# Attention's k-by-v products as two 64 by 64 matmuls in two halves of the array's columns, in place of one 128 by 128

## The reference

```python
xn = _ln(x, ln_w, ln_b)
q = xn @ Wq + bq
k = xn @ Wk + bk + (1.0 - src_mask) * -1000000.0
q = softmax(q.reshape(b, t, h, dh), axis=-1)     # over a head's features
k = softmax(k.reshape(b, t, h, dh), axis=1)      # over the tokens
v = ((xn @ Wv + bv) * src_mask).reshape(b, t, h, dh)
att = einsum('bnhd,bnhl->bhdl', k, v)            # dh x dh for each head
y = einsum('bnhd,bhdl->bnhl', q, att).reshape(b, t, d)
hh = _ln(y, ln2_w, ln2_b) * (1.0 + scale) + shift   # scale, shift from emb
return x + silu(hh) @ W_out + b_out
```

## Time and profile before

| what | value |
|---|---|
| median of 3 runs | 836.76 us (836.5 to 837.15) |
| the profiled execution's own time | 837.29 us |
| its span, first to last instruction | 835.5 us |
| PE busy | 795.3 us, 95% |
| DVE, ACT, POOL busy | 691.0, 514.5, 432.1 us |
| mean granted TensorE clock | 0.986 |

### The profile page before, as it was taken

How to read it: one execution, slowest core, us unless ns; L and a number is a source line. 1 busy time by engine, 2 the same in 40 slices (tenths; PEclk the granted TensorE clock), 3 DMA queues, 4 the chain that set the end, 5 groups by cost and what they waited for, 6 DMA issues and landing times.

```text
span 835.5 us, 13821 instructions
## 1 busy us (share of the span) xinstructions
PE 795.3 (95%) x4871; PEld 409.6 (49%) x4871; DVE 691.0 (83%) x1409; ACT 514.5 (62%) x1004; POOL 432.1 (52%) x425
## 2 busy tenths in 40 slices
PE   4999779997999999999999999999999999999987
PEld 2446335463454555545454555555454555555453
DVE  6888767786898888998978889888888889788877
ACT  4975872852857677686866766475656566460622
POOL 2265573542664747767674654637264535534340
PEclk9999979998999999999999999999999999999999
DMA  9777297763774848868493949768593939476542
GB/s 321 261 167 226 44 255 219 130 142 120 133 174 107 157 165 161 230 121 188 94 207 95 185 135 151 191 133 184 95 207 100 178 126 174 117 139 140 89 114 76
DMA packets 291093, 130.53 MB, mean 156 GB/s; under 512 B 261296, under 2 KB 261680, under 8 KB 291024
## 3 DMA queue, kind: packets, MB, share of 16 engines
q1 hardware_dynamic: 288288, 125.27, 65.7%
q10 hardware_dynamic: 2736, 4.39, 1.5%
HBM read 47.74 MB, written 16.88 MB: 77 GB/s over the span
## 4 chain that ended last, share of the span: by engine, by line
PE 80%; DVE 11%; ACT 3%; DMA 2%; POOL 2%; issue 1%; SPq 0%; DVEq 0%; ACTq 0%; POOLq 0%
PE ring L500 72%; PE att_ps L500 4%; DMA sb_ht_parts<-sb_htok 1%; DVE sb_k_or_qt L976 1%; ACT sb_k_or_qt L1350 1%; DVE sb_q_sum L1033 1%; DVE sb_row_peak L823 1%; DMA sb_x<-in_x 1%; DVE sb_q_max L1009 1%; DVE ring L1011 1%; DVE ring L1006 1%; DVE ring L1052 1%; DVE sb_y_stats L1056 1%; POOL sb_x L1573 1%; PE film_ps L582 0%
## 5 line engine op out<-in xcount | busy, mean ns | idle before, releaser
L500 PE MATMUL ring<-sb_w_hi,sb_xt_parts 128*128 128x512 f16 x1024 | 310.5, 380 | 4.7 <-DVE sb_v_or_q L991 4.7
L500 PE MATMUL ring<-sb_w_lo,sb_xt_parts 128*128 128x512 f16 x512 | 194.6, 380 | 0.0
L500 PE MATMUL ring<-sb_w_hi,sb_ht_parts 128*128 128x512 f16 x512 | 158.1, 383 | 7.5 <-DMA sb_ht_parts<-sb_htok 5.8
L500 PEld LDWEIGHTS ring<-sb_w_hi,sb_xt_parts 128*128 128x128 f16 x1024 | 100.7, 98 | 131.5 <-issue 7.7
L1582 POOL TENSOR_TENSOR sb_htok<-sb_ht_parts,sb_htok 128x512 f16<-128x512 f32 x60 | 74.9, 1270 | 149.6 <-ACT sb_htok L1384 149.6
L500 PE MATMUL ring<-sb_xt_parts,sb_w_hi 128*128 128x512 f16 x496 | 147.8, 380 | 0.0
L1598 POOL TENSOR_TENSOR sb_tanh<-sb_v_or_q,sb_kq_hi 128x512 f16<-128x512 f32 x64 | 74.1, 1157 | 88.7 <-ACT sb_kq_hi L1414 88.2
L500 PE MATMUL ring<-sb_w_lo,sb_ht_parts 128*128 128x512 f16 x256 | 98.0, 383 | 0.0
L500 PE MATMUL ring<-sb_xt_parts,sb_w_lo 128*128 128x512 f16 x248 | 94.0, 379 | 0.0
L1045 DVE SCALAR_TENSOR_TENSOR sb_x<-ring,sb_down_o,sb_x 128x512 f32<-128x512 f32 x64 | 47.0, 749 | 47.1 <-PE ring L500 44.6
L500 PEld LDWEIGHTS ring<-sb_w_hi,sb_ht_parts 128*128 128x128 f16 x512 | 50.9, 99 | 67.1 <-issue 10.6
(11 more groups left out here) (228 smaller groups left out, 1477.1 us busy)
## 6 DMA issues: line engine op xcount, KB each, us to landing
out<-sb_x SPq DMA_DIRECT2D x14, 1024.0 KB, 4.4
sb_rows_now<-film_rows SPq DMA_DIRECT2D x16, 512.0 KB, 4.7
sb_x<-out SPq DMA_DIRECT2D x8, 1024.0 KB, 5.4
sb_x<-in_x SPq DMA_DIRECT2D x7, 1024.0 KB, 5.6
sb_mask_add<-mask_terms SPq DMA_DIRECT2D x15, 256.0 KB, 5.6
sb_w_stage<-in_L_cond_Wk SPq DMA_DIRECT2D x2, 1024.0 KB, 8.4
sb_w_hi<-in_L_cond_W_emb SPq DMA_DIRECT2D x1, 1536.0 KB, 13.0
sb_w_lo<-in_L_cond_W_emb SPq DMA_DIRECT2D x1, 1536.0 KB, 13.9
```

Source lines behind the costliest of these rows:

```text
L500: last = nc.tensor.matmul(out, lhs, rhs, start=(n == 0), stop=(n == len(pairs) - 1))
```

## The change

For the units 1 to 15 `attention` calls a new function in place of `product`. For each of the 12 pairs of operands it issues two matmuls: one takes the first 64 features of k and of v and writes the upper left 64 by 64 square of the block, the other takes the last 64 and writes the lower right one. The output partition (0 or 64) places them in the first and the second half of the array's columns. The other two squares of the block are no longer written in these units; they keep what the tensor held, and the multiplication by `blocks` takes them to zero as before. In a unit 48 loads of 128 columns with 48 matmuls of 128 columns become 96 loads of 64 columns with 96 matmuls of 64 columns. In layer 0 the stationary operand is k and the moving one v, in layer 1 the other way round, before and after. Nothing is moved: the order of all other instructions, the semaphores and the waits stay.

```diff
+HALF = P // 2
@@
+            def pairs_of_heads(c, pairs):
+
+                for n, (lhs, rhs) in enumerate(pairs):
+                    for j in range(2):
+                        g = slice(j * HALF, j * HALF + HALF)
+                        last = nc.tensor.matmul(att_ps[g, c, g], lhs[:, g], rhs[:, g], start=(n == 0), stop=(n == len(pairs) - 1))
+                return last
+
             def attention(u):
@@
                     left, right = (k_parts, v_parts_t) if layer_of(u) == 0 else (v_parts_t, k_parts)
-                    last = product(att_ps[:, c, :], split_pairs(*left, *right))
+                    last = pairs_of_heads(c, split_pairs(*left, *right))
                 last.then_inc(att_summed, 1)
```

## The result

The changed kernel is **faster** by 0.55%, a little, but clear of the noise: 832.51 us median of 7 runs (830.5 to 834.82) against 836.76 for the kernel before (7 runs, 835.73 to 838.75); the ratio is 0.9945, 95% interval 0.9926 to 0.9964. The forecast was 841.0 us, slower. The rival "half-width fp16 loads are quick" had said 823.5. So the sign was missed, and the rival that had the sign right promised three times as much as came.

A forecast was written before the change was run, and what follows sets the result against it. PE's unbroken chain of matmuls was taken as the bound. Attention was to go from 2.68 to 2.97 us a unit, said as +0.30; 14 units add 4.2 us, giving a median of 841.0 us, range 823 to 846.

The forecast's parts named there:

- half-width fp16 loads are quick: Rival for attention's loads: 0.43 ns a column, rounds of 31 ns, -0.95 us a unit, 823.5 us; chance 0.27.
- The bound and the units: PE's unbroken chain sets the end; each ns of attention counts in 14 of the 15 changed units.
- What costs nothing: Mask multiplication, cast and low part after attention: 0.3 us later, covered by 10.4 us of output matmuls.
- The halves at once: In attention, two 64-column tiles run fully in parallel, so a unit takes 48 rounds.
- What does a load of 64 columns take?: Attention's 64-column load sets each round: 56 to 58 ns, taken as 57.
- the fp32 end: Attention's fp16 loads were taken at the fp32 loads' 0.86 ns a column.
- What the pages gave for the load: By the skill pages, a 64-column load in attention takes 53 ns, so a round is at least that and nothing is gained.
- Going in and out: Switching to and from narrow tiles around attention costs 0.09 us in and 0.10 us out; lower bound 0.
- The sum for the kernel: 14 units times 0.30 us give 4.2 us more over the whole kernel; median 841.0 us.
- One after another: Rival: attention's 96 pairs run serially at 0.056 us each, +2.9 us a unit, 855 to 878 us; chance 0.12.
- doesn't show: Rival: attention rounds of 56 ns and switch costs only with fp32, 836.8 to 837.5 us; chance 0.09.
- 831 us of a slower issue: Weaker form of the quick-load rival: attention's instructions issue at some 12 ns, 2.3 us a unit, kernel near 831.

The follow-up runs named there:

- one place: Changed kernel, but layer 0 sends both 64-column halves to the same half of the array's columns and layer 1 uses four 32-column quarters; 861.64 us.
- The run with 32 and 64 fp16 columns: Changed kernel, but layer 0 loads 64 columns and streams 32, while layer 1 loads 32 and streams 64; 831.32 us.
- one turn less: Changed kernel with the later peak sums, but in units 1 to 15 a plain transfer replaces the turn of q's low part; 824.92 us, 0.9841.
- later peak sums: Changed kernel, with the matmuls summing a weight's peak behind the fourth output tile instead of the third in units 3 to 6; 828.68 us, again 829.60.
- block order: Changed kernel, but layer 0 issues the first half's 12 matmuls ahead of the second half's, and layer 1 streams all 128 columns per half; 840.39 us.

## Why the prediction was wrong

**The bound and the units.** That PE's chain sets the end was right for the kernel before; that each ns won in 14 units would arrive was wrong, and for the slower forecast it didn't matter. The part "What costs nothing" looked at mask, cast and low part of attention only, and named no room for what else runs beside it. It is there that a gain needs a row: how much earlier than needed does each other operand of the next step arrive?

**The halves at once: right.** 3.15 us in one place, 1.64 in two.

**What does a load of 64 columns take? This is the step that failed.** It took "the fp32 end", 0.86 ns a column and a round of 57 ns, "because today's short load is a feature of a full-width load". The run with 32 and 64 fp16 columns shows 0.47 ns a column, and the round is 31.5 ns. The value between the ends, 0.43 "if fp16 is simply twice as fast as fp32", was near it. The rows had the hint: the prediction itself says that fp16 streams at 0.42 ns a column and fp32 at 0.84. That the narrow loads of the earlier trace rows "all stand on the one line of 0.86" was true, but all of them are fp32. The reading of 16 ns for the columns of a full-width load holds: take the 15 ns of 32 columns off their load of 98 ns and 83 are left, against the 82 that the prediction had from fp32. So a full-width fp16 load lasts as long as one of 32 columns, while one of 64 columns takes 15 ns more.

**What the pages gave for the load.** The Trainium skill's page "TensorEngine Tiling (Array Packing)", section "Restrictions and Gotchas", excludes Fast Weight Load, a quicker way of loading weights, under column tiling. The trace agrees in that the 64-column load (113 ns) is longer than the full-width one (98 ns). The figure of columns / 1.2 ns of the Trainium skill's page "TensorE: Matmul & The Clock Gate", section "LDWEIGHTS (loading the stationary operand)", is 53 ns for 64 columns; here the whole round is 31.5 ns. The measurement decides: 0.83 ns a column is near the fp32 loads here (0.86), not the fp16 ones (0.47). What the runs bear out is the up to twice the speed of the Trainium skill's page "TensorEngine Tiling (Array Packing)", section "Overview", which the prediction held only as a rival: 2.68 to 1.64 us is 1.6 times.

**Going in and out: right in size.** In 0.09 us; out 0.12 us in unit 7 in the chain, and in the other units 0.07 us of start-to-start distance beyond a full-width matmul. It comes with fp16 on both sides, so it isn't a matter of fp32, and its lower bound of 0 falls. The sum for a unit in the fast rival was -0.95 us; 46.80 - 45.86 is -0.94.

**The sum for the kernel.** 14 x 0.94 = 13.2 us, as that rival said. The distances from attention to attention show where the profiled execution gives it back, each against the kernel before less 0.94: 0.1 us in unit 2, 2.8 in the units 3 to 5, 0.8 in unit 7 (46.67), 0.3 in unit 8 (46.16), 1.5 in unit 9 (47.47), 0.6 in unit 11 (46.45) and 0.8 in unit 14 (51.06). That is 6.9 of 13.2. The 6.3 that are left, and the 0.45 that were won ahead of unit 2 by the clock, are the 6.8 by which the span fell. The median fell by only 4.3, as the profiled execution was the quickest of its seven and the one before lay above its median; the others' traces weren't kept, so their share can't be placed.

**The rivals.** One after another is refuted, and so is "doesn't show". The 831 us of a slower issue (which leaves out the 0.24 us of going in and out) lies near the measured time by chance: a unit's attention took 1.64 us and not 2.3. The chance of 0.27 for faster was low for a step whose value was chosen between ends of 8 and 55 ns. The range of 823 to 846 held the time; it is the direction that was wrong.

**What stays open.** That the turning transfers bind behind unit 6 is shown, as one less brings every unit from 8 to 13 to 45.86 us. It isn't shown whether it is SyncE's time to issue them or the DMA engines' work that would have to shrink: the run with one turn less takes away both. A full-accuracy kernel with fewer turns wasn't tried. The version that beats both kernels with all of the computation is the changed kernel with the later peak sums, 828.7 and 829.6 us in two sets of runs, 0.990 of before.

## What to carry to other kernels

When an operation's cost lies between two ends, look for the same factor in a neighbouring row (here fp16 against fp32 in the stream) before taking either end. A gain on the bounding engine arrives only up to the room that every other chain of the loop has: write that room down, in us, for each operand of the next step, and expect the rest to come back as waits. And test a repair on the old kernel too: one that is worth little there and 4 us on the new one names what the change uncovered.

## What the runs showed of the hardware

Two column halves take loads and matmuls side by side, 96 pairs in 1.64 us, 17 ns a pair. Four quarters don't scale on: 192 pairs took 1.79 us at best in the chain, 9.3 ns a pair, so issue can keep up with at least that; in two of eight units a hole of some 3.5 us stood in the middle. A load of 32 fp16 columns lasts 98 ns, one of 64 columns 113, and one of all 128 again 98. Matmuls for an idle half can pass some that wait for the busy half (2.46 us in block order, against 3.15 in one place and 1.64 alternating). The granted clock stayed at 1.00 through attention in the changed kernel:

```profile
419.23:420.94 1.71, 1.71 (x97) 1.60 (x96) 1.64 (x3) 1.16 (x3) 1.64 (x2) 1.00 1.10 249
```

This is the row of the changed kernel for attention of unit 7: stretch, us, busy of PE, PEld, DVE, ACT and POOL, then PEclk, DMA share and GB/s.
